# Routing twelve of sixteen tiles of the last expert stage inside the attention before it, and starting both attentions in another order

## The reference, cut to what matters

```python
x = x + 0.5 * ffn0(norm(x))     # mixture of experts, 8 experts, capacity 256, 128 hidden
x = x + linear_attention(norm(x))   # 16 heads of 8, gated running state
x = x + 0.5 * ffn0(norm(x))
x = x + 0.5 * ffn1(norm(x))     # mixture of experts, 8 experts, no capacity, 512 hidden, gelu
x = x + softmax_attention(norm(x))  # 16 heads of 8, all keys in the softmax, mask after it, own norm
x = x + 0.5 * ffn1(norm(x))     # the last expert stage

def ffn1(h):                    # h: 2048 tokens
    probs = softmax(h @ Wr)     # 8 columns
    e, p_max = argmax(probs), max(probs)
    return p_max * (gelu(h @ W1[e] + b1[e]) @ W2[e] + b2[e])
```

## Time and profile before

| | us |
|---|---|
| median of 3 runs | 896.49 |
| lowest, highest | 895.97, 900.06 |
| the profiled execution, its own time | 895.41 |
| its span, from the first to the last instruction | 893.7 |
| busy in the span: PE, DVE, ACT, POOL | 677.6, 574.2, 451.4, 330.0 |
| granted TensorE clock, mean over the span | 0.866 of full speed |

### The profile page before, as it was taken

How to read it: one execution, slowest core, us unless ns; L and a number is a source line. 1 busy time by engine, 2 the same in 40 slices (tenths; PEclk the granted TensorE clock), 3 DMA queues, 4 the chain that set the end, 5 groups by cost and what they waited for, 6 DMA issues and landing times.

```text
span 893.7 us, 14258 instructions
## 1 busy us (share of the span) xinstructions
PE 677.6 (76%) x4580; PEld 350.9 (39%) x4580; DVE 574.2 (64%) x1112; ACT 451.4 (51%) x858; POOL 330.0 (37%) x767
## 2 busy tenths in 40 slices
PE   4275777645419937699999999999999999930993
PEld 4162322634408924123333333342333433320893
DVE  5446799735624455778787887879887894050343
ACT  2145401224106625047777677867777678810661
POOL 0633465064533422621423233242523443206242
PEclk9998889568559977569999999999999999965897
DMA  8251930025131015610100202020100000002203
GB/s 293 74 164 37 292 47 1 0 90 158 39 86 31 26 51 148 160 44 2 38 18 10 47 2 54 1 55 1 46 11 2 2 2 2 2 3 65 65 28 100
DMA packets 56857, 51.31 MB, mean 57 GB/s; under 512 B 6080, under 2 KB 46732, under 8 KB 56528
## 3 DMA queue, kind: packets, MB, share of 16 engines
q1 hardware_dynamic: 52096, 42.19, 17.7%
q0 software_dynamic: 4544, 7.60, 3.1%
q10 hardware_dynamic: 144, 0.61, 0.2%
HBM read 30.04 MB, written 21.80 MB: 58 GB/s over the span
## 4 chain that ended last, share of the span: by engine, by line
PE 56%; DVE 19%; issue 8%; POOL 6%; DMA 5%; ACT 5%; SPq 0%; POOLq 0%; ACTq 0%; DVEq 0%
PE PS L1028 13%; PE PS L970 11%; PE PS L995 11%; PE PS L756 5%; PE PS L767 5%; DVE ARENA L1714 4%; DMA ARENA<-slots_x 2%; POOL slots_x L1777 2%; DVE PS L1654 1%; DVE ARENA L1665 1%; PE PS L641 1%; DVE XN L1305 1%; DVE STATS L1278 1%; ACT ARENA L1243 1%; PE PS L651 1%
## 5 line engine op out<-in xcount | busy, mean ns | idle before, releaser
L1714 DVE TENSOR_REDUCE ARENA<-PS 128x1 f32<-128x1024 f32 x256 | 300.9, 1219 | 60.3 <-PE PS L970 59.5
L1243 ACT ACTIVATE ARENA<-PS 128x512 f32<-128x512 f32 x512 | 272.7, 609 | 73.1 <-PE PS L995 67.9
L970 PE MATMUL PS<-ARENA 72*128 72x512 bf16 x512 | 163.3, 403 | 8.3 <-DVE ARENA L1714 5.8
L995 PE MATMUL PS<-ARENA 75*128 75x512 bf16 x512 | 162.7, 385 | 0.0
L1028 PE MATMUL PS<-ARENA 128*8 128x128 f32 (+8 forms) x1920 | 151.3, 430 | 1.0 <-POOL ARENA L1866 0.6
L1866 POOL TENSOR_SCALAR_AFFINE_SELECT ARENA<-ARENA 128x128 f32<-128x128 f32 x256 | 74.3, 295 | 144.1 <-ACT ARENA L1243 143.8
L1614 DVE TENSOR_TENSOR ARENA<-PS,ARENA 128x512 f32<-128x512 f32 x46 | 31.8, 692 | 83.9 <-PE PS L756 83.9
L995 PEld LDWEIGHTS PS<-ARENA 75*128 75x128 bf16 x512 | 47.6, 98 | 90.9 <-ACT ARENA L1243 41.1
L970 PEld LDWEIGHTS PS<-ARENA 72*128 72x128 bf16 x512 | 42.7, 99 | 92.1 <-DVE ARENA L1714 38.9
L706 PE MATMUL PS<-C,ARENA 128*128 128x128 f32 x110 | 22.0, 343 | 73.1 <-DMA ARENA<-slots_x 73.1
L1028 PEld LDWEIGHTS PS<-ARENA 128*32 128x32 f32 (+2 forms) x1920 | 43.3, 97 | 76.3 <-issue 40.3
(11 more groups left out here) (175 smaller groups left out, 844.0 us busy)
## 6 DMA issues: line engine op xcount, KB each, us to landing
ARENA<-q_parts SPq DMA_DIRECT2D x24, 192.0 KB
ARENA<-k_parts SPq DMA_DIRECT2D x24, 192.0 KB
ARENA<-pack_dram SPq DMA_DIRECT2D x8, 514.0 KB, 12.2
ARENA<-slots_x SPq DMA_DIRECT2D x16, 256.0 KB, 4.2
slots_y<-ARENA SPq DMA_DIRECT2D x32, 128.0 KB, 3.4
slots_x<-FILL SPq DMA_DIRECT2D x2, 1483.5 KB, 17.7
ARENA<-slots_x SPq DMA_DIRECT2D x10, 258.0 KB, 4.5
k_parts<-ARENA SPq DMA_DIRECT2D x10, 256.0 KB, 3.3
```

Source lines behind the costliest of these rows:

```text
L970: ins = nc.tensor.matmul(PS[:, slot + c, :], Q3[0:KQ, G % Q3R, g, i * P:(i + 1) * P], K3[0:KQ, G % Q3R, g, c * 512:(c + 1) * 512], start=T ...
L995: nc.tensor.matmul(PS[:, bank, 0:w], K3[0:MR + 3, G % Q3R, i, j * P:(j + 1) * P], Q3[0:MR + 3, G % Q3R, i, half * 512:half * 512 + w], sta ...
L1243: nc.scalar.activation(PT[:, n % NPT, 0:w], PS[:, bank_of[x], 0:w], ACT.Exp).then_inc(b_exp, 1)
L1714: nc.vector.tensor_reduce(NM[:, k % 4, i:i + 1], PS[:, slot:slot + 2, :].rearrange("p b n -> p (b n)"), AX.X, ALU.max, negate=True).then_i ...
```

## The change

- The last stage routes in two parts, tiles 0 to 11 and 12 to 15. What the first part needs is put into the attention's list behind steps 115 to 123 (`ROUTING`): three turns (X), three sets of logits (L), each copied out of PSUM by DVE, the choice (R 0), the counts (C), the slots (R 1), and four of the twelve scatters (P). The other eight follow on GpSimd when its part of the list is done, and the last four when the second part is routed. X, L and C take banks of B's ring.
- After the attention, PE turns only chunk 3, and ACT copies only that chunk.
- GpSimd adds beta to X not before its list but in it, a chunk each behind V 20, 22, 36 and 38.
- In the softmax attention's start, chunk 2 and chunk 3 go one after the other through norm, turn and projection (`block_of`), and the first group's q and k come in two pairs of heads. Statistics of chunk 3 move behind the first four splits on DVE.
- In the linear attention's start, ACT takes the first block's features before it copies chunk 1, DVE makes chunk 3's statistics after its first pass and the norms of chunks 2 and 3 after its second and third, and PE makes values before it turns chunks 2 and 3. The later projections move between passes.
- One square root on ACT stands behind the last gelu of the first ffn1 stage. A constant of 128 columns becomes two of 96 and 32.

The core of the diff (lines of semaphore bookkeeping and of arguments handed through are left out):

```diff
-PARTS = (HALVES, HALVES, HALVES, ((0, T),))
+PARTS = (HALVES, HALVES, HALVES, ((0, 12), (12, T)))
 ZSTEPS = [GR // 2 * NS + Z0 + n for n in range(16)] + [3 * GR // 4 * NS + Z0 + n for n in range(9)]
+ROUTING = {115: (("X", 0, 0),), 116: (("L", 0, 0), ("X", 1, 0)), 117: (("L", 1, 0), ("X", 2, 0)),
+           118: (("L", 2, 0), ("R", 0, 0)), 120: (("C", 0, 0), ("R", 1, 0)), 122: (("P", 0, 0), ("P", 1, 0)),
+           123: (("P", 2, 0), ("P", 3, 0))}
+SENT = 4
+BETAS = (20, 22, 36, 38)
...
+        plan += ROUTING.get(m, ())
...
-            elif x[0] in "BM":
+            elif x[0] in "BMXLC":
...
+        def block_of(n):
+            return (n % 2, n // 2) if n < 4 else (n // 2, n % 2)
...
+                def load_first(w, h):
+                    src, dst = (qd, kd)[w], (Q3, K3)[w]
+                    heads = slice(heads_of(0).start + 4 * h, heads_of(0).start + 4 * h + 3, 2)
+                    sp.wait_ge(parts_stored[0][w], (3, 5)[w] * 16)
+                    for c in range(3):
+                        a = c if w else 0
+                        rows = src[heads, a:a + 3, :, 0:S].rearrange("g a d n -> (a d) g n")
+                        sp.dma_start(dst[3 * DH * c:3 * DH * (c + 1), 0, 2 * h:2 * h + 2, :], rows
+                                     ).then_inc(ring_loaded[0] if h else pair_loaded, 16)
...
-                load_q(0)
-                load_k(0)
+                load_first(0, 0)
+                load_first(1, 0)
+                load_first(0, 1)
+                load_first(1, 1)
...
-                    turn(0)
-                    turn(1)
-                    logits(0)
-                    turn(2)
-                    logits(1)
-                    logits(2)
                     turn(3)
                     logits(3).then_inc(logits_done, 1)
-                    counts(k, 0)
+                    counts(k, 1, 3, 0)
...
-                values(0)
-                values(1)
-                for c in range(2, 4):
-                    turn(c)
-                    gates(c)
-                for n in range(4, 8):
-                    features(n)
                 for n in range(B * DH):
-                    if n >= 2:
-                        values(n)
+                    values(n)
+                    if n in (3, 4):
+                        turn(n - 1)
+                        gates(n - 1)
+                    if n in (5, 6):
+                        features(2 * n - 6)
+                        features(2 * n - 5)
...
-                turn(2)
-                turn(3)
-                for n in range(4, 8):
-                    projected(n)
+                for c in range(2, 4):
+                    turn(c)
+                    projected(2 * c)
+                    projected(2 * c + 1)
...
+                    elif kind == "X":
+                        pe.wait_ge(xn_ready, T * 5 + 4 * k + 4)
+                        for t in range(4):
+                            ins = nc.tensor.transpose(PS[:, bank, t * P:(t + 1) * P], XN[:, 4 * k + t, 0:P], ident)
+                        ins.then_inc(xt_turned, 1)
+                    elif kind == "L":
+                        pe.wait_ge(xt_copied, 4 * 5 + k + 1)
+                        for t in range(4):
+                            ins = nc.tensor.matmul(PS[:, bank, t * E:(t + 1) * E],
+                                                   XNT[:, (4 * k + t) * P:(4 * k + t + 1) * P], col("f1_wr"),
+                                                   start=True, stop=True)
+                        ins.then_inc(logits_done, 1)
+                    elif kind == "C":
+                        counts(3, 0, bank, 0)
...
-                for c in range(T // 4):
+                for c in range(3 if after_soft else 0, T // 4):
...
+                if k == 2:
+                    nc.scalar.activation(ROOT1[:, :], EPS1[:, :], ACT.Sqrt)
...
-                for c in range(2):
-                    std(c)
-                    turned(c)
-                for n in range(4):
-                    feature(n)
+                std(0)
+                turned(0)
+                std(1)
+                feature(0)
+                feature(1)
                 gate(0)
+                turned(1)
+                feature(2)
+                feature(3)
                 gate(1)
...
+                std(2)
                 for n in range(4):
                     first_part(n)
-                std(2)
+                turned(2)
+                first_part(4)
+                first_part(5)
                 std(3)
-                turned(2)
                 turned(3)
-                for n in range(4, 8):
-                    first_part(n)
+                first_part(6)
+                first_part(7)
...
-                inverse(2, number)
-                write_xn(2)
-                norm(3, before_norm(3))
-                write_xn(3)
...
-                    if 3 <= n < 7:
-                        feature_map(n + 1)
+                    if n in (6, 7):
+                        feature_map(2 * n - 8)
+                        feature_map(2 * n - 7)
...
+                    if n == 0:
+                        numbers[3] = variances(3, before_norm(3))
+                    if n in (1, 2):
+                        inverse(n + 1, numbers[n + 1])
+                        write_xn(n + 1)
...
-                numbers += [variances(c, before_norm(c)) for c in range(2, 4)]
+                numbers.append(variances(2, before_norm(2)))
...
-                for c in range(2, 4):
-                    inverse(c, numbers[c])
-                    write_xn(c)
+                inverse(2, numbers[2])
+                write_xn(2)
+                norm(3, before_norm(3))
+                write_xn(3)
...
+                    elif kind == "X":
+                        dve.wait_ge(xt_turned, 4 * 5 + k + 1)
+                        nc.vector.tensor_copy(XNT[:, k * 512:(k + 1) * 512], PS[:, bank_of[x], :]).then_inc(xt_copied, 1)
+                    elif kind == "L":
+                        dve.wait_ge(logits_done, part_number(3, 0) + k)
+                        nc.vector.tensor_copy(LG[:, 4 * k:4 * k + 4, :],
+                                              PS[:, bank_of[x], 0:4 * E].rearrange("p (t e) -> p t e", e=E)
+                                              ).then_inc(logits_taken, 1)
+                    elif kind == "R" and k == 0:
+                        chosen(3, 0, taken=True)
+                    elif kind == "R":
+                        slots1(3, 0, bank_of["C", 0, 0], 0)
...
-                    for t in range(a, b):
-                        pool.indirect_dma_start(sx[k], bass.IndirectOffsetOnAxis(ap=SCATI[:, t:t + 1], axis=0),
-                                                XN[:, t, :], None, bounds_check=NT * P - 1, oob_is_err=False
-                                                ).then_inc(scattered, 16)
+                    for t in range(SENT if k == 3 and p == 0 else a, b):
+                        scatter(k, t)
...
-                pool.wait_ge(xn_ready, T * 5)
-                for c in range(T // 4):
+                def beta_to(c):
+                    pool.wait_ge(xn_ready, T * 5)
...
+                    if kind == "P":
+                        pool.wait_ge(slots_filled[3], 16)
+                        pool.wait_ge(index_ready, part_number(3, 0))
+                        scatter(3, k)
+                    if kind == "V" and k in BETAS:
+                        beta_to(BETAS.index(k))
```

More of the change, by code:

```diff
@@ L674, in norm_turned @@
                         logits(2)
-                        counts(k, 0)
+                        counts(k, 0, 3, 0)
                     else:
-                        counts(k, 0)
+                        counts(k, 0, 3, 0)
                         turn(3)
@@ L965, in soft @@
                         G, g = divmod(k, 4)
-                        if G not in begun:
+                        if k == 0 and G not in begun:
+                            begun.add(G)
+                            pe.wait_ge(pair_loaded, 16 * 6)
+                        if k == 2 or k >= 4 and G not in begun:
                             begun.add(G)
@@ L1753, in _, with scatter @@
         def _(pool):
+            def scatter(k, t):
+                pool.indirect_dma_start(sx[k], bass.IndirectOffsetOnAxis(ap=SCATI[:, t:t + 1], axis=0),
+                                        XN[:, t, :], None, bounds_check=NT * P - 1, oob_is_err=False
+                                        ).then_inc(scattered, 16)
             def moe(kind, k):
@@ L1812, in soft @@
                 for n in range(4, 8):
-                    w, four = n // 2 % 2, slice(S + n % 2 * 512, S + (n % 2 + 1) * 512)
+                    c, w = block_of(n)
+                    four = slice(c * 512, (c + 1) * 512)
                     pool.wait_ge(part0_done, n + 1)
```

81 lines of the change are left out of this document (50 added, 31 removed).

## The result

| | before | after |
|---|---|---|
| median (runs) | 898.27 us (4) | 886.98 us (4) |
| lowest, highest | 895.97, 901.53 | 884.02, 893.92 |
| profiled execution, own time | 895.41 | 884.02 |
| its span | 893.7 | 882.2 |
| DVE busy in the span | 574.2 | 591.6 |

The ratio is 0.9882, with a 95% interval of 0.9844 to 0.9920: 1.2% or some 11 us faster, where 16.7 us were forecast. The changed kernel was timed twice more beside the experiments: 0.9906 (0.9870 to 0.9941) and 0.9874 (0.9838 to 0.9910).

What follows compares the result with a forecast made beforehand. Bound by matrix work in the attention and, between stages, chains of engines waiting on one another (PE 56%, DVE 19%). -16.6 + 6.3 - 6.0 - 0.4 = -16.7 us on 895.41: 878.7, named 879.5; range about 872 to 886.5, plus a microsecond above.

Steps and rivals of the forecast that it cites:

- Last stage: Behind the attention: twelve fewer scatters waited for (15.4 us), earlier square root (1.4), routing in two parts (loss 0.2); -16.6 us.
- The attention: Routing work put inside the softmax attention makes it end 6.3 us later (from 0 to 8).
- The term of PE: Attention's late steps: twelve turns and logits add 4.9 us on PE, less 0.8 of slack, leaving 4.1 us.
- the wait of V 124: Late in the attention, V of step 124 waits 2.2 us more for masks that GpSimd makes behind four scatters.
- The linear start: Start of the linear attention: first product at 82.7 instead of 90.11, DVE's idle time vanishes; -6.0 us (-7.1 to -3).
- The softmax start: Start of the softmax attention: no stall for beta, but PE's first A later, at 361.3 to 362.6; -0.4 us (-1.5 to +1.5).
- The rule that I weighed: Skill page: DVE in a two-port mode and GpSimd exclude each other; weighed for eight scatters beside chunk 3's norm, under 0.2 us.
- The "ports" rival: Last stage: scatters and DVE exclude each other, DVE's chain ends some 5 us late; 885 us, chance 0.07.
- The attention for little: Rival: V does not wait for masks, PE's slack is 1.6; the attention costs 0.5 to 3.3 us, about 875, chance 0.20.
- The late softmax start: Rival: A five us later in the softmax start, a maximum or DVE gap still to pay; about 885 us, chance 0.10.
- A last stage without gain: Rival: the experts' start is held by something other than the 16th scatter; about 895 us, no change, chance 0.04.
- a fallen clock: Rival: waits in the attention's late steps drop PE to 1.2 GHz of 2.4; +36 against -23, about 909 us, chance 0.03.

Runs made afterwards that it cites:

- experiment 6: The changed kernel with the four early scatters taken out of the attention, all twelve behind it: 894.89 us, ratio to the kernel before 0.9925.
- Experiment 3: The changed kernel with GpSimd's first three products in the linear attention waiting for DVE's norm work of chunks 2 and 3: 880.63 us, ratio to the kernel before 0.9811.

## Why the prediction was wrong, point by point

- **Last stage (-16.6 forecast, -17.2 measured).** Right in its steps: scatters -15.5 (-15.4 forecast), root -1.4 (as forecast), routing of four tiles as a second part -0.2 (+0.2 forecast). One reason in it was superfluous: the four early scatters bring at most 0.5 us (experiment 6).
- **The attention (+6.3, +4.4).** The term of PE was right: 4.1 forecast, 4.2 measured. The failing term is the wait of V 124, put at 2.2 us, which is 0.3 by the trace and 0.44 by experiment 6. I took GpSimd's delay for V's delay. The eight masks of two steps run at their own 0.25 us once they are late, and PE was late too.
- **The linear start (-6.0, +0.7).** Here the prediction failed most. Its step: "The norm work that stood between (4.70 us busy) is still DVE's, now between passes", at unchanged durations. Between passes is where GpSimd multiplies. The gain ahead of the first product (6.1 us) and of the idle time behind it was real, and 6.3 us of it were lost by the hold. Experiment 3 gives them back with the same instructions: from chunk 2's last statistics (the aggregate) to the ninth product there are 48.75 us in the kernel before, 49.22 in the change and 43.34 there, 5.4 less than before. So without the hold the forecast of -6.0 would have been nearly right; the first product came at 84.00, 1.3 us behind its forecast.
- **The softmax start (-0.4, +1.7).** The same step failed: chunk 3's output at 1.1 us took 4.20. Two more things were missing. The turns no longer wait for ACT's copy, which in the old order brings 2.9 us and in the new one half of it. And SP's queue is a second limit for the first B: the kernel before was at both limits at once, 25 + 4.84 us behind its first A and 22.3 us behind its last late part, so freeing GpSimd of the betas could not bring B forward by itself. Against the old order with the same turns, the new one puts the first A back by 10 us (30 to 40 behind the first update) and the first B by 5.4.
- **The rule that I weighed.** In this trace, a DVE instruction is held for 2.1 to 3.1 us when its operands lie in SBUF and GpSimd's instruction reads and writes SBUF: `tensor_scalar` from X to XN, `scalar_tensor_tensor` with two inputs from SBUF. It is not held with one input from PSUM: products (1.21) and scans (2.29) ran beside GpSimd's product at their usual length. The Trainium skill's page "SBUF — State Buffer" (section Who interferes with whom) says: with at most one SBUF input and outside the two-port modes DVE does not contend with GpSimd; with two SBUF inputs it does, against a GpSimd instruction that reads SBUF; and `tensor_scalar`, which has one, is among those that can enter a two-port mode. This trace agrees, with 2.73 us for 0.61 and 3.23 for 1.11; which mode `tensor_scalar` ran in, no trace shows. I cited the rule and applied it only to the eight scatters, where it does not bite: the two groups of four `scalar_tensor_tensor` beside them kept 1.14 us each. (The norm output there, 1.11 us at 795.14, begins only after the eighth scatter.) The place to apply it was the norm work that the change moves beside GpSimd's arithmetic. The "ports" rival had the right mechanism at the wrong place, and its 885 came out by accident.
- **The rivals.** The attention for little: the missing mask wait was right, the greater slack of PE wrong; no row stands behind the lower end of its 0.5 to 3.3 us. The late softmax start: A was late by 2 to 3 us against my forecast. A last stage without gain, and a fallen clock: no, the granted clock was 1.00 from step 115 to T.

## What to carry to other kernels

When an edit moves an instruction, look at what the *other* SBUF engine does at its new place, not only at whether its own engine is free there; in this case DVE instructions with two SBUF inputs, and `tensor_scalar` from SBUF to SBUF, stood beside GpSimd's arithmetic for the whole remaining length of its instruction. If the two must share a stretch, let GpSimd wait for DVE: it cost next to nothing here and gave 6 us. And ask, for small transfers that someone waits for, which bulk transfers the same queue has been given first: that limit stays hidden until the first one is lifted.

## What was unexpected in the hardware

- The hold follows GpSimd's instruction, 2.35 us for 1024 columns, or the late parts' instructions in a row (4.20 us for four outputs that take 1.11 us alone).
- GpSimd's scatters do not hold DVE in that way: four norm outputs beside scatters took 1.24 us and 1.29 us in experiment 6, against 1.11 without.
- Masks that were late ran 0.25 us apart, twice as fast as ACT delivers their inputs; here GpSimd's queue made up most of its delay by itself.
